# Degrees of a sorted edge list from counts of the destinations, seven nodes per tile, with a second pass of the sort where they do not hold

## What is computed

```python
src = jnp.concatenate([_s, _d, _loop])
dst = jnp.concatenate([_d, _s, _loop])
_o = jnp.argsort(dst, stable=True)
src = src[_o]; dst = dst[_o]
...
s, t = edge_index[0], edge_index[1]          # src, dst
qe = q[s] * scale + (edge_attr @ q_rpe_w + q_rpe_b)
ke = k[t] + (edge_attr @ k_rpe_w + k_rpe_b)
ve = v[t] + (edge_attr @ v_rpe_w + v_rpe_b)
compat = einsum('ehd,ehd->eh', qe, ke)
attn = softmax of compat over the edges with the same s
out = segment_sum(ve * attn, s)
return layernorm(x + out)
```

## Time and profile before

| | us |
|---|---|
| median of three runs | 5160.68 |
| the profiled execution | 5161.2 |
| its span, first to last instruction | 5159.5 |
| PE busy | 4163.8 (81%) |
| DVE busy | 4326.1 (84%) |
| ACT busy | 3195.1 (62%) |
| POOL busy | 3600.9 (70%) |
| mean granted clock of PE | 0.584 of 2.4 GHz |

### The profile page before, as it was taken

How to read it: one execution, slowest core, us unless ns; L and a number is a source line. 1 busy time by engine, 2 the same in 40 slices (tenths; PEclk the granted TensorE clock), 3 DMA queues, 4 the chain that set the end, 5 groups by cost and what they waited for, 6 DMA issues and landing times. The chain is left out here.

```text
span 5159.5 us, 104272 instructions
## 1 busy us (share of the span) xinstructions
PE 4163.8 (81%) x21690; PEld 3684.9 (71%) x21690; DVE 4326.1 (84%) x18393; ACT 3195.1 (62%) x7804; POOL 3600.9 (70%) x3778
## 2 busy tenths in 40 slices
PE   5657988888888888888888888888888888758886
PEld 4546877777777777777777777777777777647765
DVE  8997988888888888888888888888888888669997
ACT  6985766666666666666666666666666666525555
POOL 0005777777777777777777777777777777768876
PEclk8995555555555555555555555555555555579998
DMA  3103444444444444444444444444444444679996
GB/s 90 32 0 123 146 128 130 129 128 130 128 129 129 128 130 129 128 130 129 129 130 128 128 131 128 130 129 128 129 129 128 130 128 128 147 285 379 361 337 225
DMA packets 377939, 756.08 MB, mean 147 GB/s; under 512 B 142015, under 2 KB 205830, under 8 KB 364984
## 3 DMA queue, kind: packets, MB, share of 16 engines
q1 hardware_dynamic: 254050, 381.31, 26.2%
q0 software_dynamic: 123808, 373.89, 20.2%
HBM read 567.24 MB, written 187.60 MB: 146 GB/s over the span
## 5 line engine op out<-in xcount | busy, mean ns | idle before, releaser
L627 POOL DMA_INDIRECT rec_dram<-recs,place_i x3232 | 3124.8, 967 | 1012.0 <-issue 972.3
L775 PE MATMUL ps_feat<-w_in,edge_in 51*128 51x128 f32 x6464 | 1655.2, 434 | 625.3 <-ACT recs L786 624.8
L775 PEld LDWEIGHTS ps_feat<-w_in,edge_in 51*128 51x128 f32 x6464 | 1436.7, 325 | 800.8 <-issue 717.1
L758 PE MATMUL ps_look<-free_rec,lo_hotT 128*128 128x98 f32 x6464 | 1608.8, 431 | 1.6 <-ACT lo_hotT L799 1.6
L661 DVE SCALAR_TENSOR_TENSOR matches<-ids_b,src_f,ps_const 128x128 bf16<-128x128 int16 (+3 forms) x3232 | 1567.9, 538 | 0.1
L758 PEld LDWEIGHTS ps_look<-free_rec,lo_hotT 128*128 128x128 f32 x6464 | 1472.3, 333 | 1.8 <-ACT lo_hotT L799 1.8
L786 ACT ACTIVATE recs<-ps_feat 128x512 f32<-128x512 f32 x808 | 481.2, 596 | 1485.2 <-DMA rec_dram<-recs,place_i 1481.9
L681 DVE TENSOR_TENSOR place_i<-first,rank 128x4 int32<-128x4 f32 x808 | 131.3, 162 | 709.6 <-ACT recs L786 708.9
L670 DVE CUSTOM_DVE_ANT_0 picked<-hi_hot,ps_look 128x98 f32<-128x98 bf16 x3232 | 628.3, 248 | 1.0 <-PE ps_look L758 1.0
L793 ACT ACTIVATE lo_hotT<-ids_b,minus_p 128x512 f32<-128x512 int16 x808 | 575.0, 712 | 5.0 <-DMA w_in<-kv_dram 5.0
L799 ACT ACTIVATE lo_hotT<-lo_hotT,one 128x512 f32<-128x512 f32 x808 | 569.6, 705 | 0.0
(11 more groups left out here) (171 smaller groups left out, 3598.5 us busy)
## 6 DMA issues: line engine op xcount, KB each, us to landing
ids_b<-id_dram SPq DMA_DIRECT2D x808, 384.0 KB
rec_dram<-recs,place_i POOLq DMA_INDIRECT x3232
edge_in<-in_attr SPq DMA_DIRECT2D x808, 36.0 KB
w_in<-kv_dram SPq DMA_DIRECT2D x808, 12.0 KB
qx_dram<-qx SPq DMA_DIRECT2D x1, 4753.0 KB, 41.5
kv_dram<-dig_i SPq DMA_DIRECT2D x14, 336.0 KB, 2.6
xt<-in_xT SPq DMA_DIRECT2D x14, 224.0 KB, 3.3
qx<-qx_dram,node_i POOLq DMA_INDIRECT x98, 7.0
```

Source lines behind the costliest of these rows:

```text
L627: pool.indirect_dma_start(rec_dram[:, :], bass.IndirectOffsetOnAxis(place_i[j][:, m:m + 1], 0), recs[j][:, m, 0:ROW], None).then_inc(scatt ...
L758: last = nc.tensor.matmul(ps_look[j % NS][:, m, 0:NB], lo_hotT[j % NS][:, P * m:P * (m + 1)], free_rec[j % 2][:, :], start=True, stop=True)
L775: last = nc.tensor.matmul(ps_feat[j % 2][:, m, :], edge_in[j][0:K_ROWS, tile], w_in[j][0:K_ROWS, :], start=True, stop=True)
```

## The change

The count of destinations is used instead of the count of sources. The list is sorted by destination, so a tile of 128 edges has few nodes, in order. Seven columns stand for the nodes from the tile's first destination (`NEAR = 7`): DVE writes destination minus first destination (`near`), then one-hots of seven columns for all tiles in 51 instructions (`near_hot`), and 101 matmuls with a picking row sum them to one count per tile and column (`ps_count`, 101 x 224). The 224 columns are then put where they belong in the 128 x 98 table, by 14 groups of 16 products of a one-hot and a scaled one-hot. Copies and the 32-node windows move to ACT and POOL; the windows come from the first destination of each unit. PE's 98 node tiles stand after the counts: 14, then 7 behind each of 12 groups.

The sort always runs its windowed loop. It counts the sources anyway (`ps_cnt`), so behind it DVE compares that count with `deg`; every engine reads the flag, and if it is set, all make the degrees again and run the general loop over all units. A row that is taken from wrong degrees is kept inside the buffer (a minimum with `EP`), which has 512 spare rows.

```diff
-            def one_hots(g, i):
...
-                dve.tensor_tensor(h_lo[i][:, :, :, :], value[:, :, :].unsqueeze(1).broadcast_to((P, PAIRS, P, 2)), tiles(lo_w, PAIRS, P),
-                                  ALU.is_equal)
-                dve.tensor_tensor(h_hi[i][:, :, :, :], value[:, 0:NB, :].unsqueeze(1).broadcast_to((P, HPAIRS, NB, 2)), tiles(hi_w, HPAIRS, NB),
-                                  ALU.is_equal).then_inc(one_rows, 1)
+            step(dve.tensor_tensor(near[:, :], dst_t[:, :], origin[:, :], ALU.subtract))
+            for g in range(GROUPS):
...
+                dve.tensor_tensor(near_hot[g % NG][:, 0:tiles // 2, :, :],
+                                  offset[:, :, :].unsqueeze(1).broadcast_to((P, tiles // 2, NEAR, 2)),
...
+            dve.wait_ge(ids_made, WG + 1)
+            dve.tensor_single_scalar(srcl_i[:, :, :], srcl_i[:, :, :], P - 1, ALU.bitwise_and).then_inc(split, 1)
+            dve.wait_ge(near_done, GROUPS)
+            step(dve.tensor_copy(count[:, :], ps_count[0:WP, 0:COLS]))
+            for g in range(LGROUPS):
+                if g >= 2:
+                    dve.wait_ge(hot_done, g - 1)
+                dve.tensor_tensor(lo_hots[g % 2][:, :, :, :], value[0:WP, :, :].unsqueeze(1).broadcast_to((WP, LG // 2, P, 2)),
...
+                for k in range(LG):
+                    c = LG * g + k
+                    last = dve.tensor_scalar(hi_counts[g % 2][:, k, :], iota_row[0:WP, 0:NB], node_hi[:, c:c + 1], count[:, c:c + 1],
+                                             ALU.is_equal, ALU.mult)
+                last.then_inc(hot_made, 1)
...
+            for q in range(WP):
+                g, half = q // 2, q % 2
+                if half == 0:
+                    pe.wait_ge(near_made, g + 1)
+                last = nc.tensor.matmul(ps_count[0:WP, 0:COLS], pick_row[:, P - 1 - q:P - 1 - q + WP],
...
+            node_tiles(2 * XG)
+            for g in range(LGROUPS):
+                pe.wait_ge(hot_made, g + 1)
+                for k in range(LG):
+                    c = LG * g + k
+                    last = nc.tensor.matmul(ps_hist[:, 0:NB], lo_hots[g % 2][:, k // 2, :, k % 2], hi_counts[g % 2][:, k, :],
+                                            start=(c == 0), stop=(c == COLS - 1), skip_group_check=True)
+                last.then_inc(hot_done, 1)
+                node_tiles(XG)
...
-        def both_ways(eng, loop):
-
-            general = eng.value_load(flag[0:1, 0:1], min_val=0, max_val=1)
-            with eng.If(general < 1):
-                loop(eng, False)
-            with eng.Else():
-                loop(eng, True)
+        def in_doubt(eng, again):
+            eng.wait_ge(wrong_made, 2)
+            doubt = eng.value_load(flag[0:1, 0:1], min_val=0, max_val=1)
+            with eng.If(doubt > 0):
+                again(eng)
...
-            both_ways(pool, send_loop)
+            send_loop(pool, False)
+            in_doubt(pool, again_pool)
             pool.wait_ge(qx_out, 16)
...
-            both_ways(dve, vector_loop)
+            vector_loop(dve, False)
+            compare(dve)
+            in_doubt(dve, again_vector)
             by_degree(dve)
```

More of the change, by code:

```diff
@@ L431, in _, with node_tiles @@
-            with pe.Fori(NB // NG, GROUPS // NG) as it:
-                for i in range(NG):
-                    tally(NG * it + i, i)
+            done = 0
+            def node_tiles(n):
+                nonlocal done
+                for b in range(done, min(done + n, NB)):
+                    g, i = b // XG, b // XG % 2
+                    if b % XG == 0:
+                        pe.wait_ge(x_in[i], 16 * (g // 2) + 16)
+                        if g >= 2:
+                            pe.wait_ge(x_read, g - 1)
+                    last = nc.tensor.matmul(ps_x[i][:, b % XG, :], xt[i][:, b % XG * P:(b % XG + 1) * P], w_qkv[:, :],
+                                            start=True, stop=True)
+                    if b % XG == XG - 1:
+                        last.then_inc(x_done, 1)
+                done = min(done + n, NB)
@@ new lines, in _ @@
+            act.wait_ge(win_set, 1)
+            for g in range(WG):
+                act.activation(dst_loc[:, g, :], dst_l[:, g, :], ACT.Identity, bias=minus_win[:, g:g + 1]).then_inc(ids_made, 1)
+            act.wait_ge(srcl_in, 32)
+            act.activation(src_lin16[:, :, :], srcl_i[:, :, :], ACT.Copy).then_inc(ids_made, 1)
+            tables(0)
+            tables(1)
+            act.wait_ge(split, 1)
+            act.activation(lo_f[:, :], lo_i[:, :], ACT.Copy).then_inc(narrowed, 1)
@@ L490, in sort_stage @@
+            act.wait_ge(split, 2)
+            act.activation(hi_f[:, :], hi_i[:, :], ACT.Copy).then_inc(narrowed, 1)
+            act.wait_ge(split, 3)
+            act.activation(lo_lin[:, :, :], srcl_i[:, :, :], ACT.Copy).then_inc(ids_made, 1)
+            for g in range(2, NXG):
+                tables(g)
+            act.wait_ge(narrowed, 2)
 def sort_stage(nc, T, x, attr, dst_tiles, id_dram, kv_dram, rec_dram, qx_dram):
@@ L597, in step @@
             def step(u, j, turn):
-                if starts(u, NU):
+                if starts(u, NU) and not general:
                     sp.wait_ge(slots_set[j], 2)
                 else:
-                    sp.wait_ge(ranked, u - NU + 1)
-                    sp.wait_ge(feats, u - NU + 1)
+                    sp.wait_ge(ranked, z + u - NU + 1)
+                    sp.wait_ge(feats, z + u - NU + 1)
                 at_u = bass.ds(u, 1)
@@ L655, in ranks @@
             def ranks(u, j, turn):
-                if not starts(u, NS):
-                    dve.wait_ge(ranked, u - NS + 1)
-                dve.wait_ge(loaded[j], LOADS[general] * turn + LOADS[general])
+                if general or not starts(u, NS):
+                    dve.wait_ge(ranked, z + u - NS + 1)
+                dve.wait_ge(loaded[j], LOADED[general] + LOADS[general] * turn + LOADS[general])
                 for m in range(CT):
@@ new lines, in again_vector, with step @@
+        def again_vector(dve):
+            n = 6
+            def step(ins):
+                nonlocal n
+                n += 1
+                ins.then_inc(wrong_steps, 1)
+                dve.wait_ge(wrong_steps, n)
+            step(dve.tensor_copy(deg[:, :], true_deg[:, :]))
+            step(dve.memset(beyond[:, :], 1.0))
+            step(dve.tensor_tensor_scan(incl[:, :], beyond[:, :], deg[:, :], 0.0, ALU.mult, ALU.add))
+            step(dve.tensor_tensor(column[:, :], incl[:, :], deg[:, :], ALU.subtract))
+            dve.sem_inc(true_sums, 1)
+            dve.wait_ge(true_rows, 1)
+            step(dve.tensor_copy(real[:, :], ps_look[0][:, 0, 0:1]))
+            dve.tensor_scalar(base[:, :], column[:, :], real[:, 0:1], None, ALU.add).then_inc(true_based, 1)
+            passes_by_tile(dve, 1)
+            dve.wait_ge(true_based, 1)
+            vector_loop(dve, True)
```

535 lines of the change are left out of this document (271 added, 264 removed).

## The result

The changed kernel takes **4845.9 us** (median of four runs, 4844.09 to 4847.42); the kernel before took 5160.9 beside it. The ratio is 0.9394, with a 95% interval of 0.9382 to 0.9405. The forecast was 4876 us, with a range of 4854 to 4910: the sign came as told, and the time lies 30 us under the forecast and 8 us under the low end.

A forecast was written before the change was run, and what follows sets the result against it. The first stage was taken as bound by DVE's one-hots, the sort by POOL's sends. 5161.2 us, less 288.5 for the first stage, plus 4 for POOL's load and branch, less 0.5 for the median, gave 4876 us; range 4854 to 4910.

The forecast's parts named there:

- The bound and the account by stages: Whole kernel: DVE's one-hots bound the first stage, POOL's sends the sort; the last send sets when the last stage begins.
- From first to last send 4129 us again: Sort's loop: 3232 sends on POOL keep their pace of 1.27 us each, so the loop's length does not change.
- Loads at 15.4: First stage: the 3.3 MB that `near` needs, at 215 GB/s, are ready at 15.4 us.
- `near` 3.6, `near_hot` and the products 15 to 18, the digits: First stage: `near` 3.6 us, `near_hot` 15.3 on DVE, its products 18.4 on PE, two digits 3.7.
- 0.12 us for a scaled one-hot: First stage's groups: each 98-element scaled one-hot takes DVE 0.12 us, so 3.1 us a group, 2.1 to 3.9.
- DVE waits for PE in the groups: First stage's groups: DVE needs 3.1 us, PE 5.3 cold or about 3.0 warm; 4.4 taken, with DVE waiting.
- The stage, -288.5: First stage: `base` is done at 109.9 us instead of 398.4, so 288.5 us less.
- Rival A: First stage's groups: PE at the high clock, DVE's 3.1 us sets the pace, 4861 us; chance 0.20.
- Rival B: First stage: low clock throughout, pace 5.3, 4887 us; stalls of straight-line code give up to 4907; chance 0.20.
- +4 for POOL's load and branch: Behind the last send: POOL's flag load and branch delay the gathers by 4 us, between bounds +1.2 and +10.7.
- Rival C: Behind the sort's loop: the result is in doubt and the sort is redone, about 13,100 us; chance 0.02.
- Rival D: Slower head of the sort, or order by degree later than POOL, takes up to some 30 us of gain; chance 0.08.

The follow-up runs named there:

- Experiment 1: The kernel before, always with the windowed loop, without the flag's load and the general loop: 5157.2 us, ratio 0.9997.
- Experiments 6 and 7: First: kernel before plus one small arithmetic instruction on POOL, 5133.1 us. Second: changed kernel with `win_row` worked out by DVE instead of POOL, 4874.9 us.
- Experiment 4: The changed kernel with a group's 16 scaled one-hots made by two wide DVE instructions, counts and node digits in bf16: 4838.2 us, ratio 0.9380.
- experiments 1 and 12: Experiment 1, and the changed kernel without comparison, flag, jumps and the loop that does the sort over: the latter 4849.5 us, ratio 0.9401, on its rerun.
- experiment 8: The kernel of Experiment 4 with the sources' narrow copy on POOL instead of ACT and 28 node tiles, not 14, ahead of the groups: 4841.1 us.
- experiments 8 and 11: experiment 8, and the kernel of Experiment 4 with an addition of two tiles on POOL besides: the latter 4839.0 us, ratio 0.9377, on its rerun.

## Why the prediction was wrong, point by point

- **The bound and the account by stages: right.** The sort starts when `base` is there, and the last send sets when the last stage begins. Experiment 1 bears it out for the sort's end: 10.4 us off DVE's path there change nothing.
- **"From first to last send 4129 us again": wrong, and the one step that put the time outside the range.** I wrote that the forecast is wrong if the pace moves off 1.27 us a send, on which the rest of the sum rests, and then gave that no chance and no width. By its own sum (busy time and "issue", over 3232) the pace was 1.268 and is 1.263; from the first start to the last it was 1.278 and is 1.269 us a send. Rounded to 1.27 the miss can't even be seen, and 3232 times it is 28 us. I had looked at which instructions change inside the loop and costed them at nothing, rightly: the idle time ahead of the sends is 1012.0 us in both. What changed the sends stands 120 us ahead of it: `win_row`, moved to POOL. Experiments 6 and 7 put it at 27.0 us (5160.2 - 5133.1) and 29.0 (4874.9 - 4845.9). The second difference is across chips; the ratios, 0.9451 and 0.9394, give the same.
- **Loads at 15.4: too late.** `near` starts at 12.02. The 215 GB/s was the mean of a stretch of which the first 5 us moved 176 GB/s and the next 307; 272 GB/s was moved now in the first 20 us.
- **`near` 3.6, `near_hot` and the products 15 to 18, the digits: right** (3.52; 16.26; 1.84 each). The fourteen short steps took 6.3 us (31.76 to 38.1), not 4: the first of them alone has a row of 2.85, beside POOL's cast, which the prediction did not look at. The sum ahead of the groups has a slip of 0.3 (36 + 4.8 + 3.7 is 44.5 and not 44.8). The first group starts at 45.95 against 47.5.
- **0.12 us for a scaled one-hot: mis-sized.** It is 0.22, and 3.54 for sixteen. The nearest row was of another operation, and 0.17 of it, start to start, was nearer than what I took. With 1.1 for the wide one-hot the group is 4.59, outside my 2.1 to 3.9 for DVE. The pace taken, 4.4, came out near 4.59 by luck: it was a mean of two clocks for PE, and DVE set the pace. PE needs 4.43 at the low clock and not 5.3, since seven tiles take 3.11 us and not 3.6, and the 16 products 1.32 and not 1.6.
- **DVE waits for PE in the groups: wrong.** DVE sets the pace. Experiment 4, which makes DVE's part 3.1 as forecast, turns it round: 4.43 a group and 1.31 of waiting for PE.
- **The stage, -288.5:** -283.5 measured, 5 us short. The groups take 66.0 us (45.95 to 111.90) and not 59.1: thirteen intervals of 4.59, and the last two groups, without node tiles, run at that too and not at 1.6. Their start was 1.5 earlier, and the closing sums 0.4 shorter, than told.
- **Rival A (high clock through the groups): fell.** PE is at the low clock from 40 us on. The clock fell while PE was idle and did not come back, granted 0.50 at 20.00 of 20 us busy, in the groups (also where PE sets the pace, experiment 4) as in the sort. The sentence of the Trainium skill, "TensorE: Matmul & The Clock Gate", Part 1, that sustained activity releases the low clock is contradicted here; the trace decides. By the rows of DVE the high clock would have been worth little in the changed kernel anyway (an estimate: 4.59 a group for DVE, whatever PE does).
- **Rival B:** its half about the clock is what happened and cost nothing, because PE needs 4.43 a group there and not 5.3, less than DVE. Its half about stalls of straight-line code did not come: DVE has no idle stretch in the groups.
- **+4 for POOL's load and branch: wrong, 0.** The step failed in the words "now it can't be". I took a branch that depends on a late flag to be taken late. The flag was there at 4200.7, and POOL's sequencer, 14 us ahead of its engine, read it at 4215.3. A wait in the sequencer shorter than that lead is hidden. DVE paid 9.12 us at its own jump, as forecast. The section "Instruction fetch mechanics" of the Trainium skill's "Runtime: NRT & Kernel Launch" describes such a fetch stall. The trace agrees with it on DVE, as far as an idle stretch that ends in "issue" and goes with the branch (experiments 1 and 12) can, and shows nothing of it on POOL, where it would have been covered.
- **Order by degree 7 us ahead of POOL:** right, `node_i` is there at 4220.9, nearly 10 ahead of the first gather.
- **Rival C, the redo:** did not happen. **Rival D** named something that I hadn't thought of, on the wrong side only.
- **The last stage:** 613.6 us against 617.3. In the runs at the usual pace it goes from 609.8 (experiment 4) to 621.0 (experiment 8), with nothing changed in that stage, so 3.7 us are no effect that can be told.

Without the send's 28 us the forecast would have stood at 4848 against 4846. That nearness is luck: it holds an error of 5 us one way (the first stage) and of 4 (POOL's branch) and 3.7 (the last stage) the other.

## What to carry to other kernels

When one instruction runs thousands of times on the engine that sets the pace, its own duration is a term of the sum with a width: here 1% of it was worth 28 us, against the 5 us by which the account of a stage written anew was off. Before saying that a loop is untouched, look at what its engine runs ahead of it too, and compare that instruction's mean duration in both traces first. And ask of a branch not when its flag is written, but how far ahead of its engine the sequencer is: a stall there is free as long as work is queued.

The fastest kernel here is the changed one with wide scaled one-hots, 4838.2 us; experiments 8 and 11, built on it, are not told apart from it.

## What the runs showed of the hardware

- One arithmetic instruction on GpSimd, of a kind that it had not run yet (a minimum with a constant over 404 or 808 numbers, or a sum of two tiles of 64), makes the indirect DMAs that it issues later shorter: 958 ns for 967, through all 3232 of them, 4.1 ms long. With memsets, iotas, selections, copies and casts alone the sends stay at 967, one more cast included, and a second new kind adds nothing. The gathers that it issues behave alike, 952 ns ahead of its first arithmetic and 944 behind, within one execution of the kernel before. The first send becomes a little longer, 1.16 us to 1.20 with the minimum (1.17 with the sum). No run shows why arithmetic does this, and it stays open.
- Small VectorE operations beside a cast on GpSimd ended with the cast: 2.85 us for one of 101 x 8 numbers, and 3.47 where the same operation took 0.18 before the cast was moved beside it (experiment 8). Moving work to GpSimd is not free for VectorE.
- TensorE's clock fell from 1.00 to 0.50 in an idle stretch of 15.34 us, and stayed at 0.50 through the 60 us of work behind it (busy 20.00 of 20 us from 60 to 100) and in the sort.
- The same kernels took 5952 us on one of the chips for the kernel before and 5158 to 5161 on the others, with instructions of nearly the same length and more idle time between them.
